# Graph attention layer on one core: the Newton steps of two groups of layer-norm roots moved from VectorE to GpSimd, and their statistics moved ahead of the weight products

## The reference

```python
h = jnp.maximum(_layernorm(x, axis=-1), 0.0)      # (x - mean) / sqrt(var + 1e-5), then relu
Wh = h @ W_w + W_b                                # 8192 x 256
e = leaky_relu((Wh @ a1)[:, None] + (Wh @ a2)[None, :], 0.2)
attention = softmax(where(adj > 0, e, -9e15), axis=1)   # adj is 8192 x 8192 int32
out = x + attention @ Wh
```

## Time and profile before

| | |
|---|---|
| median of three runs | 1481.46 us |
| the profiled execution | 1480.05 us, span 1478.0 us |
| TensorE (PE) | busy 98% of the span |
| VectorE (DVE) | busy 98% of the span |
| ScalarE (ACT), GpSimd (POOL) | busy 75% and 59% |
| the head | first 104 us |

### The profile page before, as it was taken

The page is one execution under the profiler, slowest core; times in us unless marked ns, Lnnn a source line. Parts: engine busy times, 40 slices in busy tenths (PEclk is TensorE's granted clock), DMA queues, the critical chain, the costliest instruction groups (busy, mean ns, idle before and its releaser), DMA issues.

```text
span 1478.0 us, 30023 instructions
## 1 busy us (share of the span) xinstructions
PE 1445.3 (98%) x12686; PEld 1255.3 (85%) x12686; DVE 1444.0 (98%) x1288; ACT 1107.2 (75%) x1040; POOL 876.2 (59%) x1218
## 2 busy tenths in 40 slices
PE   6979999999999999999999999999999999999998
PEld 4858888888888888888888888888888888888887
DVE  8989999999999999999999999999999999999996
ACT  5868888688876888777786878767776888768881
POOL 4758174597547774497636974486745975479000
PEclk9979999999999999999999999999999999999999
DMA  9749499529982689709984499717995299826600
GB/s 220 83 39 98 76 95 73 41 38 117 102 60 31 82 96 89 51 16 123 98 66 30 58 117 96 53 23 108 92 78 40 39 117 102 60 30 84 60 1 29
DMA packets 179574, 107.53 MB, mean 73 GB/s; under 512 B 20080, under 2 KB 176368, under 8 KB 179440
## 3 DMA queue, kind: packets, MB, share of 16 engines
q0 software_dynamic: 155904, 75.56, 64.5%
q1 hardware_dynamic: 23536, 30.05, 6.9%
HBM read 298.45 MB, written 8.42 MB: 208 GB/s over the span
## 4 chain that ended last, share of the span: by engine, by line
PE 81%; DVE 16%; issue 2%; ACT 1%; DMA 0%; POOL 0%; SPq 0%; DVEq 0%
PE acc L883 80%; DVE work L709 4%; DVE work L702 4%; DVE adj_cols L628 2%; DVE xr L486 1%; DVE X L533 1%; PE acc L844 0%; ACT work L397 0%; DVE xr L497 0%; DVE xr L528 0%; DVE work L780 0%; DVE xr L518 0%; DVE xr L810 0%; PE acc L870 0%; DVE xr L522 0%
## 5 line engine op out<-in xcount | busy, mean ns | idle before, releaser
L883 PE MATMUL acc<-X,work 128*128 128x257 f16 x12288 | 1361.9, 273 | 8.4 <-DVE work L785 4.3
L883 PEld LDWEIGHTS acc<-X,work 128*128 128x128 f16 x12288 | 1189.7, 97 | 181.0 <-issue 7.2
L300 POOL DMA_DIRECT2D adj_rows<-in_adj x1024 | 559.4, 782 | 351.0 <-DVE adj_cols L628 328.7
L412 ACT ACTIVATE work<-work 128x2048 f16<-128x2048 f32 x254 | 484.1, 1908 | 170.4 <-DVE work L702 117.9
L702 DVE SCALAR_TENSOR_TENSOR work<-work,sigma,adj_cols 128x2048 f32<-128x2048 f32 x254 | 595.4, 2344 | 4.4 <-ACT work L397 0.9
L709 DVE SCALAR_TENSOR_TENSOR work<-work 128x2048 f16<-128x2048 f32 x254 | 593.8, 2338 | 5.3 <-ACT work L412 5.3
L397 ACT ACTIVATE work<-q_odd,r_j 128x1024 f32<-128x1024 f32 x256 | 279.9, 1140 | 76.3 <-DVE work L709 76.1
L397 ACT ACTIVATE work<-work,r_j 128x1024 f32<-128x1024 f32 x252 | 275.3, 1140 | 62.7 <-DVE work L709 62.4
L628 DVE STREAM_TRANSPOSE adj_cols<-adj_rows 128x512 int32<-128x512 int32 x256 | 176.0, 696 | 1.3 <-PE acc L870 1.3
L315 POOL TENSOR_SCALAR part_mean<-mean_hw,rows_without_edge 128x256 f32<-128x256 f32 x56 | 144.3, 2577 | 8.9 <-POOL xr L317 7.5
L317 POOL TENSOR_TENSOR xr<-xr,part_mean 128x256 f32<-128x256 f32 x56 | 124.7, 2226 | 4.7
(11 more groups left out here) (85 smaller groups left out, 129.7 us busy)
## 6 DMA issues: line engine op xcount, KB each, us to landing
adj_rows<-in_adj POOLq DMA_DIRECT2D x1024, 64.0 KB, 9.5
xr<-in_x SPq DMA_DIRECT2D x16, 512.0 KB, 9.1
xr<-in_L_gnn_W_b POOLq DMA_DIRECT2D x16, 512.0 KB, 15.5
out<-xr SPq DMA_DIRECT2D x15, 512.0 KB, 3.0
work<-in_x SPq DMA_DIRECT2D x28, 256.0 KB, 14.6
work<-q_rows SPq DMA_DIRECT2D x4, 512.0 KB, 7.3
q_odd<-q_rows SPq DMA_DIRECT2D x4, 512.0 KB, 7.3
work<-in_x SPq DMA_DIRECT2D x8, 128.0 KB, 3.2
```

What stands on the lines that cost most here:

```text
L300: pool.dma_start(rows8[QP * q:QP * (q + 1), n % R8], adj_v[s, m, k, q]).then_inc(s_rows[n % R8], 16)
L412: nc.scalar.mul(Et[:, at:at + 2, 0, :], Wt[:, i % RING], SCALE).then_inc(s_H, 1)
L883: return nc.tensor.matmul(acc[:, m, 0:F1], Et[:, 2 * (k % RING) + e, 1 if n == 2 else 0, m * P:(m + 1) * P], X16[:, 2 * k + e, 1 if n == 1 ...
```

## The change

The Newton steps of groups 1 and 2 go to GpSimd. VectorE makes the variance plus epsilon and the first guess (function guesses, two instructions) and raises root_guesses_ready. [...] The statistics and the guess of group 1 move ahead of the products of W with a. Two waits come in where a group's mean and variance slots are used again (groups 3 and 4), and one that keeps norm_factors_ready in order.

```diff
+    BY_GPSIMD = (1, 2)
...
+            def roots(g, k):
+                pool.wait_ge(s_seed, k + 1)
+                at, lo, hi, b = GROUPS[g]
+                n = 4 * (hi - lo)
+                y, a, v = rstd[:, b:b + n], pool_a[:, 0:n], pool_vs[:, k, 0:n]
+                mean_x = mv[:, b % XG:b % XG + n, 0]
+                for turn in range(3):
+                    root_op(a, y, y, ALU.mult)
+                    root_op(a, a, v, ALU.mult)
+                    root_scale(a, a, -0.5, 1.5)
+                    root_op(y, y, a, ALU.mult)
+                root_op(a, mean_x, y, ALU.mult)
+                nc.gpsimd.tensor_scalar(shift[:, b:b + n], a, -1.0, 0.0, ALU.mult, ALU.add).then_inc(s_norm, 1)
+
             for b in range(4, NB):
+                for k, g in enumerate(BY_GPSIMD):
+                    if b == GROUPS[g][3]:
+                        roots(g, k)
                 normalise(b)
...
                 dve.wait_ge(s_bn, b + hi)
+                if lo == 0 and g in (3, 4):
+                    dve.wait_ge(s_norm, g - 1)
...
                     elif k == STEPS - 1:
+                        if g:
+                            dve.wait_ge(s_norm, g)
...
+            def guesses(g, k):
+                b, n = of_group(g)
+                dve.wait_ge(s_var, b + n)
+                pool_v = pool_vs[:, k, 0:n]
+                step(nc.vector.tensor_scalar(pool_v, mv[:, b % XG:b % XG + n, 1], EPS, None, ALU.add))
+                nc.vector.tensor_scalar(rstd[:, b:b + n].bitcast(I32), pool_v.bitcast(I32), -0.5, RSQRT_SEED,
+                                        ALU.mult, ALU.add).then_inc(s_seed, 1)
+
             def first_groups():
                 stats(0, 0, 4)
                 norms_at_once(0)
+                stats(1, 0, 4)
+                variances(1, 0, 4)
+                guesses(1, 0)
                 dve.wait_ge(s_par, 16 * (KF + 2))
...
-                stats(1, 0, 4)
-                norms_at_once(1)
...
                         variances(g, each * n, each * n + each)
-                        for k in range(STEPS):
-                            root_step(g, k)
+                        guesses(g, 1)
```

More of the change, by code:

```diff
@@ L122, in gat_layer @@
         newt = scratch[:, 1552:1568]
+        pool_vs = scratch[:, 1696:1712].rearrange("p (k n) -> p k n", k=2)
+        pool_a = scratch[:, 1712:1720]
         rstd = scratch[:, 1568:1632]
@@ L171, in gat_layer @@
         s_norm = sem("norm_factors_ready")
+        s_seed = sem("root_guesses_ready")
+        s_proot = sem("gpsimd_root_steps")
         s_h = sem("h_ready")
@@ L322, in add_bias, with root_op, root_scale @@
                                accum_op=ALU.add).then_inc(s_xb[half], 16)
+            proots = [0]
+            def root_op(out, in0, in1, op):
+                proots[0] += 1
+                nc.gpsimd.tensor_tensor(out, in0, in1, op).then_inc(s_proot, 1)
+                pool.wait_ge(s_proot, proots[0])
+            def root_scale(out, in0, mul, add):
+                proots[0] += 1
+                nc.gpsimd.tensor_scalar(out, in0, mul, add, ALU.mult, ALU.add).then_inc(s_proot, 1)
+                pool.wait_ge(s_proot, proots[0])
+            def roots(g, k):
[11 more added lines that the diff above has]
+                nc.gpsimd.tensor_scalar(shift[:, b:b + n], a, -1.0, 0.0, ALU.mult, ALU.add).then_inc(s_norm, 1)
             for b in range(4, NB):
+                for k, g in enumerate(BY_GPSIMD):
+                    if b == GROUPS[g][3]:
+                        roots(g, k)
                 normalise(b)
@@ L502, in root_step @@
                 b, n = of_group(g)
+                before = (STEPS - 1) * (g - len(BY_GPSIMD) if g else 0)
                 a, v, y = newt[:, 0:n], var[:, 0:n], rstd[:, b:b + n]
@@ L508, in root_step @@
                 else:
-                    dve.wait_ge(s_root, (STEPS - 1) * g + k)
+                    dve.wait_ge(s_root, before + k)
                     if k == 1:
```

## The result

The changed kernel takes 1484.59 us, the median of 13 runs (1481.25 to 1485.65), against 1479.91 for the kernel before (13 runs, 1479.78 to 1481.63). The ratio is 1.0023, with a 95% interval of 1.0016 to 1.0030: slower by 3.4 us, 2.4 to 4.4. The two medians themselves lie 4.7 us apart, because both sets of runs fall in groups and a median jumps between them; where the text says "by the ratio" it means the 3.4. The profiled execution took 1482.64 us (span 1480.6) against 1480.05, 2.6 more; it is the third fastest of the 13, and what the slower ones may have in addition is told at the end of the experiments and in the account of the prediction.

What follows compares the result with a forecast made beforehand. VectorE was taken to bound the head, TensorE its end. Late factors gave +1.3 us, the fallen clock 2.0: +3.3 on the 1480.75 mean gives 1484.0, range 1480.0 to 1488.0.

Steps and rivals of the forecast that it cites:

- The waits before pair 2: VectorE waits 0.7 us for group 1's load, then for TensorE's sum until 17.8; 0.7 of 4.0 us saved is left.
- The time of a root step: Each of fourteen GpSimd operations takes t = 0.30 us with handoff, 4.2 us a group.
- A rival's number: Quick GpSimd, chance 0.18: t from 0.18 to 0.21, VectorE never waits at pair 4, 1480.0 us.
- 0.7 us in hand: What VectorE keeps of its 4.0 us saved when pair 2 begins at 21.5 in place of 22.2.
- 14 x t - 2.9: Shift of the head in us for time t of one GpSimd operation, never under -0.7.
- The slack and the wait: At pair 4's L528: slack 2.3 us before; block 8 at 25.9 makes VectorE stand 2.0, head 1.3 later.
- The break-even at t = 0.21: The change neither gains nor loses if one GpSimd root operation takes 0.21 us.
- The clock: TensorE's clock falls in a 4.3 us pause before block 8; pair 3 and block 9's transposes take 2.0 us more.
- The main part keeps its length: The part after the head is unchanged and only starts earlier or later as the head ends.
- the late factors: GpSimd's roots of group 2 delay block 8 and pair 4's L528: +1.3 us if the clock holds, chance 0.28.

Runs made afterwards that it cites:

- split: The kernel before with only the third Newton turn and the shift of group 2 on GpSimd: 1480.58 us, ratio 0.9998.
- six turns: The changed kernel with six Newton turns in place of three for group 2 on GpSimd: 1487.16 us, ratio 1.0049.
- fill of 6: The changed kernel with 6 matmuls, results never read, in TensorE's pause ahead of block 8's transposes: 1481.86 us, ratio 1.0012.
- third set: Last of three sets of follow-up runs, each with its own runs of the kernel before, whose median here was 1481.65 us.
- products first: The changed kernel with the products of W ahead of group 1's statistics again, both groups' roots on GpSimd: 1481.73 us, ratio 1.0008.
- warm, changed: The changed kernel with 22 identity matmuls ahead of the first transposes and further fills, to keep TensorE at work: 1481.63 us, ratio 1.0008.
- warm, before: The kernel before with 22 identity matmuls ahead of the first transposes and 3 matmuls ahead of block 8: 1480.49 us, ratio 1.0003.

## Why the prediction was right

The forecast was +3.3 us; the ratio gives +3.4, the head of the profiled execution +2.55. The forecast time of 1484.0 lies near the 1484.59 measured by two errors that cancel in part: it starts from 1480.75, 0.8 over the median that the kernel before has in 13 runs, and the medians rise by 4.7, not by 3.3.

- *The waits before pair 2.* Load at 9.96 forecast, VectorE started at 9.98; first projections 1.6 later forecast, 1.54 measured; sum at 17.8 forecast, 17.4 measured, since the projections took 3.32 and not 3.57, and pair 2 began at 20.98 (forecast 21.5). The wait that the prediction put at over 1 us was 0.76, because VectorE had come later to it: one wait was not in the sum, the load of group 2 (1.34 us), and it cost nothing more, since TensorE's sum came last.
- *The time of a root step.* 0.30 forecast, 0.286 measured; 4.2 and 4.0 us for group 2. It lies inside the bounds from the memset and the select (0.18 and 0.54), in their lower half. The estimate from the figures of the Trainium skill, "GPSIMD Engine Reference" (section Performance versus the Vector engine), t near 0.16, was too low, as the earlier trace rows had hinted.
- *A rival's number.* For t from 0.18 to 0.21 the prediction lets the whole 0.7 us in hand stay. Its own formula gives 14 x t - 2.9, that is -0.4 to 0. So the lower end of the range, 1480.0, should have stood at 1480.4 to 1480.8 by that rival. Nothing in the result turns on it.
- *The slack and the wait.* Block 8 forecast for 25.9, it came at 25.16. Without a fall the step at 28.65 would have come at 25.16 + 2.05 + 1.76 + 0.22 = 29.2, + 0.5. The slack of 2.3 us is borne out by the split, which stays inside it and does not wait, and by six turns, whose added 3.4 us come out at the end and more. The break-even at t = 0.21 was not run.
- *The clock.* Forecast with 0.42: it falls in the pause, and the projections of pair 3 take 1.8 us more. It fell, and they took 1.5 more (3.28 from 27.33 to 30.61). With the second transposes it is 1.8 of the 2.36 us by which VectorE's step is late (31.01 against the 29.2 above), the larger part. The fill of 6 takes the half rate away: the step comes 1.05 earlier, although block 8 stands 0.2 later there and the fill itself takes 0.4. But the reason given for the fall leant on a pause of 4.3 us, and the pause was 2.90: TensorE ended pair 2 at 22.98 and not at 22.2, since it had waited 0.82 for block 5, and block 8 came early. The runs have pauses of 2.0 and 2.25 us that brought a fall and of 2.0 and 2.37 that did not, so the fall behind 2.90 was not certain, and this step came right in part by luck.
- *The main part.* "The main part keeps its length" is the step that may have failed. It holds for the profiled execution (1374.3 in both), but 8 of the 13 runs lie at 1484.5 or more, 1.9 to 3.0 us over the profiled one. Two things seen in the profiles would together make 1.7 to 2.5 of it. The main part is 1.7 longer in every profile with a fall at the stripes' meeting. And the profiled execution had the earliest sum of all profiles with the statistics moved up: VectorE's first step of the scale is at 17.40 there, and at 17.64 to 18.23 in the six others (two of them with fills ahead of it), up to 0.8 us later. That the eight runs are made of these is argued, since none of them was profiled. The kernel before has an upper cluster too (3 of 13 runs here, 18 of 33 in the third set), so whether the change makes it more frequent stays open.

So the total of 3.3 was met partly by chance: the head of the profiled execution lost 0.7 less than forecast, and the rest of the ratio comes from slower runs whose cause the sum did not have.

## What to carry to other kernels

A step moved off the busiest engine saves only what no other wait takes up: here 4.0 us went, and 2.9 came back as three waits in front of the next dependent point. If the moved step is on another engine's path, compare its added time with the slack there, in one number, before moving; moving six of the operations fitted and all of them did not. And a new pause of TensorE of 2 to 3 us is to be priced with the half rate that may follow, which here cost 1.8 us against the 0.5 of the late factors.

## What was not expected of the hardware

- The clock fell behind pauses of 2.0 us (at the stripes' meeting, in four of fourteen profiles) and held behind pauses of the same length in the other ten; in the head it fell behind 2.25, 2.9, 3.67 and 6.70 us of pause, and in the two warm runs behind 1.50 and 1.65 us, and held behind 1.45 (before) and 2.37 (split). So the length of the pause alone does not tell, below 2.4 us.
- Small dependent operations on GpSimd are very even: 0.28 to 0.30 us from start to start, tensor_tensor and tensor_scalar alike, on 8 numbers. Beside VectorE's products group 1's 14 took 4.4, and without them 4.0 (products first). Why is open.
- Small matmuls of the identity brought TensorE to full rate at 5 to 7.5 us (warm, changed: 11 matmuls in 2 to 4 us, 21 in 6 to 8), but did not hold it when TensorE worked with gaps (a clock of 0.50 in 12 to 16 us).
- A half rate of pair 1's projections cost the kernel before nothing (warm, before: 3.20 us, clock 0.50 in 18 to 20, head 79.75), and one of pair 3's cost the changed kernel 1.8 us.
